# Half 0's last expert groups taken in turns with half 1's first, and half 0's gathered rows added around the wait for the turned gates

## The reference

```
x = x + 0.5 * rwkv_ffn(layernorm(x))
x = x +       softmax_attention(layernorm(x))      # 8 heads
x = x + 0.5 * rwkv_ffn(layernorm(x))
x = x + 0.5 * experts(layernorm(x))                # "m3" in the kernel
x = x +       linear_attention(layernorm(x))       # decayed delta scan, 8 heads
x = x + 0.5 * experts(layernorm(x))                # "m5"
```

```
topk_w, topk_idx = top_k(softmax(x @ Wr + br), 2)   # 16 experts, the best 2 of each token
h = gelu(layernorm(x @ W1[e] + b1[e]) * g1[e] + be1[e])
y = sum over the 2 experts of topk_w * (h @ W2[e] + b2[e])
```

## Time and profile before

| | us |
|---|---|
| median of 3 runs | 601.48 (598.48 to 602.64) |
| the profiled execution | 601.2 |
| its span, first to last instruction | 599.0 |
| PE busy | 487.4 (81%) |
| DVE busy | 468.1 (78%) |
| ACT busy | 312.5 (52%) |
| POOL busy | 158.8 (27%) |
| mean granted PE clock | 0.925 of full |

### The profile page before, as it was taken

The page is one execution under the profiler, slowest core; times in us unless marked ns, Lnnn a source line. Parts: engine busy times, 40 slices in busy tenths (PEclk is TensorE's granted clock), DMA queues, the critical chain, the costliest instruction groups (busy, mean ns, idle before and its releaser), DMA issues.

```text
span 599.0 us, 9248 instructions
## 1 busy us (share of the span) xinstructions
PE 487.4 (81%) x2996; PEld 259.4 (43%) x2996; DVE 468.1 (78%) x1248; ACT 312.5 (52%) x613; POOL 158.8 (27%) x198
## 2 busy tenths in 40 slices
PE   6787989999999999899788789748786887789720
PEld 3452422222222232244364679535435444679610
DVE  4978898988878988465887978697977776888852
ACT  2355456777776777688232658527143202468800
POOL 5020030010000110001274702773101055630775
PEclk8888999999999999999987979987989888999975
DMA  6006500049705003000235295511000012454542
GB/s 209 3 1 162 96 2 0 19 103 194 259 2 146 2 0 72 2 0 2 67 131 163 82 277 162 154 48 27 2 1 0 2 36 68 145 166 139 155 127 66
DMA packets 55356, 49.31 MB, mean 82 GB/s; under 512 B 4958, under 2 KB 47502, under 8 KB 54926
## 3 DMA queue, kind: packets, MB, share of 16 engines
q1 hardware_dynamic: 34686, 31.15, 18.8%
q0 software_dynamic: 4240, 9.45, 5.7%
q10 hardware_dynamic: 16384, 8.13, 4.5%
HBM read 25.85 MB, written 20.59 MB: 78 GB/s over the span
## 4 chain that ended last, share of the span: by engine, by line
PE 37%; DVE 28%; POOL 11%; issue 9%; ACT 9%; DMA 4%; ACTq 1%; SPq 0%; POOLq 0%; DVEq 0%
PE ps L814 9%; DVE arena L862 8%; PE ps L804 7%; PE ps L761 7%; POOL rows_in L1157 7%; ACT arena L1357 5%; POOL arena L1173 2%; DVE stat L257 2%; ACT arena L1366 1%; POOL small L249 1%; DMA row<-in_rows 1%; PE ps L575 1%; DVE arena L1905 1%; DMA arena<-rows_in 1%; DVE xl L285 1%
## 5 line engine op out<-in xcount | busy, mean ns | idle before, releaser
L862 DVE TENSOR_REDUCE arena<-ps 128x1 f32<-128x1024 f32 x128 | 150.8, 1219 | 25.0 <-PE ps L761 24.7
L927 ACT ACTIVATE arena<-ps 128x512 f32<-128x512 f32 x256 | 138.4, 602 | 55.1 <-PE ps L804 52.8
L804 PE MATMUL ps<-arena 99*128 99x512 bf16 x256 | 85.5, 383 | 1.1 <-ACT arena L927 1.0
L761 PE MATMUL ps<-arena 96*128 96x512 bf16 x256 | 76.5, 381 | 7.0 <-DVE arena L862 6.7
L1173 POOL DMA_INDIRECT arena<-rows_out,route x64 | 61.2, 956 | 66.4 <-DMA rows_out<-arena 47.1
L1157 POOL DMA_INDIRECT rows_in<-xl,route x64 | 62.4, 976 | 55.2 <-DVE route L1113 37.1
L814 PE MATMUL ps<-arena 128*32 128x512 f32 x512 | 68.2, 605 | 1.9 <-ACT arena L923 1.3
L804 PEld LDWEIGHTS ps<-arena 99*128 99x128 bf16 x256 | 22.2, 98 | 72.9 <-ACT arena L927 48.9
L249 POOL TENSOR_TENSOR small<-small,nhalf 128x8 f32<-128x8 f32 x11 | 18.2, 1657 | 123.4 <-DVE small L271 123.3
L1357 ACT ACTIVATE arena<-ps,route 128x128 f32<-128x128 f32 x124 | 46.4, 461 | 5.7 <-PE ps L1238 5.7
L202 PE MATMUL ps<-zerob 128*128 128x512 bf16 x148 | 43.7, 448 | 1.4 <-POOL zerob L2100 1.4
(11 more groups left out here) (276 smaller groups left out, 786.6 us busy)
## 6 DMA issues: line engine op xcount, KB each, us to landing
arena<-rows_in SPq DMA_DIRECT2D x28, 256.0 KB, 4.5
rows_out<-arena ACTq DMA_DIRECT2D x28, 256.0 KB, 2.6
rows_in<-zerob SPq DMA_DIRECT2D x2, 1920.0 KB, 11.1
arena<-att_parts SPq DMA_DIRECT2D x12, 256.0 KB, 8.9
arena<-in_consts SPq DMA_DIRECT2D x2, 1024.0 KB
arena<-zerob SPq DMA_DIRECT2D x1, 2048.0 KB, 10.5
arena<-att_parts SPq DMA_DIRECT2D x14, 128.0 KB, 8.1
att_parts<-arena SPq DMA_DIRECT2D x6, 256.0 KB
```

The lines of the kernel that those rows point to most:

```text
L761: ins = pe.matmul(ps[:, bank + keys, :], a_qs[0:96, b, h, j * P:(j + 1) * P], a_ks[0:96, b, h, keys * 512:(keys + 1) * 512], start=True, s ...
L804: pe.matmul(ps[:, score_bank(n), :], a_ks[0:99, b, h0 + h4, i * P:(i + 1) * P], a_qs[0:99, b, h0 + h4, half * 512:(half + 1) * 512], start ...
L862: nc.vector.tensor_reduce(a_nm[:, o % 2, k:k + 1], ps[:, bank:bank + 2, :].rearrange("p a b -> p (a b)"), AX.X, ALU.max, negate=True).then ...
L927: nc.scalar.activation(a_p[:, n % 16, :], ps[:, score_bank(n), :], ACT.Exp, scale=0.25).then_inc(a.ex, 1)
```

## The change

In `moe_tensor` and `moe_scalar` the loop is split at group 8. Up to group 4 it is as before. Then come three rounds: on PE `out(4+k)`, `turn(5+k)`, `turn_in(8+k)`, `hidden(8+k)`; on ACT `out_in(4+k)`, `store(3+k)`, `rows(8+k)`, `gelu(5+k)`, for k = 0, 1, 2. Then half 0's last group is finished (`out(7)`, `out_in(7)`, `store(7)`) ahead of `turn_in(11)` and `rows(11)`, and half 1 goes on in the old loop. `moe_vector_tiles` takes 7 and 8 apart: each has its own chain. Both stages run this code.

Behind the groups of m3, `moe_vector_b2` is split: after the gate rows DVE adds quarters 0 and 1 of half 0's gathered rows, then copies the turned gates, adds quarters 2 and 3, and adds the b2 product last. A semaphore `b2a` tells PE that this last addition is done. On POOL the root for half 0 stands ahead of half 1's gather number 4 instead of 6. Behind m5 the order is as it was.

```diff
--- before.py
+++ after.py
@@ -1006,6 +1006,7 @@
             hot, count = sem("e_one_hot"), sem("e_counts")
             base, slot, tab = sem("e_bases"), sem("e_slots"), sem("e_tile_table")
             turned, pick = sem("e_bases_turned"), sem("e_tile_one_hot")
+            b2a = sem("e_b2_added")
             gw, gwt, gwc, gb = sem("e_gate_rows"), sem("e_gate_rows_turned"), sem("e_gate_rows_in"), sem("e_b2_by_gates")
             gs, gsel = sem("e_scales_summed"), sem("e_scales_in")
             rows_sent = [sem(f"e_rows_sent{b}") for b in range(B)]
@@ -1274,17 +1275,30 @@
             between(1)
             keep_clock(pe, HIDDEN_BANKS[3], 6)
             pe.wait_ge(pair[1].slot, pair[1].i + 1)
-            for u in range(u0, last - LEAD):
+            n = u0 + NGR
+            for u in range(u0, n - LEAD):
                 hidden(u + LEAD)
-                if u + LEAD + 1 < last and u + LEAD + 1 != u0 + NGR:
+                if u + LEAD + 1 < n:
                     turn_in(u + LEAD + 1)
                 turn(u)
                 if u == u0:
                     counts_read(pair[1])
                 else:
                     out(u - 1)
-                if u + LEAD + 1 == u0 + NGR:
+            for k in range(LEAD):
+                out(n - 4 + k)
+                turn(n - 3 + k)
+                turn_in(n + k)
+                hidden(n + k)
+            out(n - 1)
+            turn_in(n + LEAD)
+            for u in range(n, last - LEAD):
+                hidden(u + LEAD)
+                if u + LEAD + 1 < last:
                     turn_in(u + LEAD + 1)
+                turn(u)
+                if u > n:
+                    out(u - 1)
             out(last - LEAD - 1)
             turn(last - 3)
             turn(last - 2)
@@ -1306,7 +1320,7 @@
                     ins = pe.matmul(ps[:, b2_bank(m.b, q), :], r_gt[:, m.b, :], b2d[:, 4 * q:4 * q + 4, :], start=True, stop=True)
                 ins.then_inc(Moe.gb, 1)
 
-        def moe_vector_b2(dve, vs, pair):
+        def moe_vector_gate_rows(dve, vs, pair):
 
             for m in pair:
                 dve.wait_ge(m.gate, m.i + 1)
@@ -1314,6 +1328,8 @@
                     ins = nc.vector.tensor_tensor(r_oh[m.b][:, k], r_oh[m.b][:, k], bc(r_e[m.b][:, k, :].unsqueeze(2), [P, TB, NE]), ALU.mult)
                 vs.step(ins)
                 nc.vector.tensor_tensor(r_oh[m.b][:, 0], r_oh[m.b][:, 0], r_oh[m.b][:, 1], ALU.add).then_inc(Moe.gw, 1)
+
+        def moe_vector_gate_rows_in(dve, pair):
             turn = pair[1].i // B + 1
             dve.wait_ge(Moe.gwt, turn)
             nc.vector.tensor_copy(r_gt[:, :, :], ps[:, TURN_IN_BANKS[0], 0:B * P].rearrange("p (b t) -> p b t", b=B)).then_inc(Moe.gwc, 1)
@@ -1326,7 +1342,8 @@
             for q in range(2):
                 xq = x[:, TB * m.b + 4 * q:TB * m.b + 4 * q + 4, :]
                 ins = nc.vector.tensor_tensor(xq, xq, ps[:, b2_bank(m.b, q), :].rearrange("p (a b) -> p a b", a=4), ALU.add)
-            vs.step(ins)
+            ins.then_inc(Moe.b2a, 1)
+            dve.wait_ge(Moe.b2a, m.i + 1)
 
         def turn_bank(left):
 
@@ -1373,16 +1390,32 @@
             def store(u):
                 moe_scalar_store(act, pair[(u - u0) // NGR], (u - u0) % NGR)
 
-            for u in range(u0, last - LEAD):
+            n = u0 + NGR
+            for u in range(u0, n - LEAD):
                 if u >= u0 + 2:
                     store(u - 2)
-                if u + LEAD + 1 < last and u + LEAD + 1 != u0 + NGR:
+                if u + LEAD + 1 < n:
                     rows(u + LEAD + 1)
                 gelu(u)
                 if u > u0:
                     out_in(u - 1)
-                if u + LEAD + 1 == u0 + NGR:
+            for k in range(LEAD):
+                out_in(n - 4 + k)
+                store(n - 5 + k)
+                rows(n + k)
+                gelu(n - 3 + k)
+            store(n - 2)
+            out_in(n - 1)
+            store(n - 1)
+            rows(n + LEAD)
+            for u in range(n, last - LEAD):
+                if u >= n + 2:
+                    store(u - 2)
+                if u + LEAD + 1 < last:
                     rows(u + LEAD + 1)
+                gelu(u)
+                if u > n:
+                    out_in(u - 1)
             out_in(last - 4)
             store(last - 5)
             gelu(last - 3)
@@ -1432,12 +1465,13 @@
                     bc(t_rs[:, at, pos:pos + k].unsqueeze(2), [P, k, P]), ALU.mult).then_inc(t.z, 1)
 
             last = u0 + 2 * NGR - 1
-            for u in range(u0 - 1, last + 1, 2):
-                groups = range(max(u, u0), min(u + 1, last) + 1)
+            n = u0 + NGR
+            for groups in ([u0], [u0 + 1, u0 + 2], [u0 + 3, u0 + 4], [u0 + 5, u0 + 6], [u0 + 7],
+                           [n], [n + 1, n + 2], [n + 3, n + 4], [n + 5, n + 6], [n + 7]):
                 for v in groups:
                     summed(v)
                 dve.wait_ge(t.ss, groups[-1] + 1)
-                if u < u0:
+                if groups[0] == u0:
                     vs.finish_both(slots, Chain(rstds(groups[0], groups[-1])))
                 else:
                     vs.finish(Chain(rstds(groups[0], groups[-1])))
@@ -1574,6 +1608,7 @@
             def turn(self, g):
                 bank = self.bank("turn", g)
                 self.pe.wait_ge(self.m.added, 4 * self.m.i + 2 * g + 2)
+                self.pe.wait_ge(Moe.b2a, self.m.i + 1)
                 for j in range(4):
                     ins = self.pe.transpose(ps[:, bank, j * P:(j + 1) * P], x[:, TB * self.b + 4 * g + j, :], cc("ident"))
                 ins.then_inc(l.tp, 1)
@@ -2133,7 +2168,7 @@
             moe_pool_send(pool, m3[0])
             moe_pool_send(pool, m3[1])
             moe_pool_fetch(pool, m3[0])
-            moe_pool_fetch(pool, m3[1], {6: lambda: norm_pool_root(pool, n4, 0)})
+            moe_pool_fetch(pool, m3[1], {4: lambda: norm_pool_root(pool, n4, 0)})
             norm_pool_root(pool, n4, 1)
             norm_pool_root(pool, n5, 0)
             moe_pool_send(pool, m5[0], {13: lambda: norm_pool_root(pool, n5, 1)})
@@ -2298,9 +2333,11 @@
                 vs.advance(slots)
 
             def behind_m3():
-                moe_vector_b2(dve, vs, m3)
+                moe_vector_gate_rows(dve, vs, m3)
+                moe_vector_add(dve, vs, m3[0], (0, 1))
+                moe_vector_gate_rows_in(dve, m3)
+                moe_vector_add(dve, vs, m3[0], (2, 3))
                 moe_vector_b2_add(dve, vs, m3[0])
-                moe_vector_add(dve, vs, m3[0])
                 norms = Chain(norm_vector_stats(dve, vs, n4, 0, False, False))
                 for _ in range(VARIANCE_DONE):
                     vs.advance(norms)
@@ -2310,7 +2347,8 @@
             slots = lin_vector(dve, vs, m3, n4, n5, m5)
 
             def behind_m5():
-                moe_vector_b2(dve, vs, m5)
+                moe_vector_gate_rows(dve, vs, m5)
+                moe_vector_gate_rows_in(dve, m5)
                 for m in m5:
                     moe_vector_b2_add(dve, vs, m)
                 moe_vector_add(dve, vs, m5[0])
```

## The result

The changed kernel takes 604.01 us (median of 22 runs, 600.8 to 607.71) against 601.62 (22 runs, 598.13 to 603.95): ratio **1.0046, 95% interval 1.0028 to 1.0064**, by which it is 2.8 us (1.7 to 3.9) slower; the medians lie 2.4 apart. The forecast was 602.1, +0.9. Direction and mechanism came as forecast; the size did not.

What follows compares the result with a forecast made beforehand. The prediction took POOL's queue and group 15's store to bound the end: -2.5 us behind m3 and +4.1 in the second stage put half 1's gathers at 574.3 instead of 573.42, +0.9, 602.1 us; range 597.8 to 606.2.

Steps and rivals of the forecast that it cites:

- The end hangs on POOL's queue and group 15's store: Second stage's end: POOL free at 573.4, group 15's store plus 2.8 at 572.7; earlier half 0 wins at most 0.7 us.
- A round takes 4.2 us: PE and ACT, groups 5 to 7: nothing runs under gelu, so a group takes 4.2 us instead of 3.05.
- Second stage: Second expert stage: DVE 4.0 us late at group 10's statistics, last store 4.1 late; half 0's last store 0.55 earlier.
- First stage: First expert stage: group 10's statistics at 361.0 against 360.35, 0.6 us late; half 0's last store 3.9 earlier.
- Behind m3, 2.5 us earlier: After the first stage: row adds fill DVE's waits, root moves on POOL; linear attention starts at 395.9 instead of 398.44.
- The sum: Whole kernel: last store 569.88 - 2.5 + 4.1 = 571.5, half 1's gathers at 574.3; +0.9 us, 602.1.
- The additional chain costs nothing: DVE, groups 7 and 8 apart: about 3.15 us a chain, covered by the wait for hidden(10); price between 0 and 3.1.
- Rival, the clock lost in the rounds: PE at half speed in the rounds: 604.6 for one stage, chance 0.20; 607.1 for both, chance 0.05.
- Rival, half 1 is not late: PE and ACT overlap more in a round, group 10's statistics come in time: end moves -3.0, 598.2; chance 0.15.
- the gain behind m3 does not arrive: Gathers late for quarters 2 and 3, or linear attention gives it back: up to 2.5 us lost, 604.6; chance 0.10.

Runs made afterwards that it cites:

- the rounds alone: The changed kernel with `moe_vector_b2` in one piece and POOL's root ahead of gather 6, as before the change: 607.07 us, ratio 1.0099 to the kernel before.
- the tail alone: The changed kernel with PE, ACT and DVE taking groups in the old order, new only behind m3's groups: 599.93 us, 0.9953; on the third chip 682.99, 0.9989.
- rounds in stage 1 alone: The changed kernel with the old group order on PE, ACT and DVE in the second stage: 601.32 us, ratio 1.0001 to the kernel before.

## Why the prediction came out as it did

- **The end hangs on POOL's queue and group 15's store.** Right. The new last store is at 572.82, half 1's gathers start 2.87 later at 575.69, as with the 2.8 taken, and POOL would have been free at 571.3.
- **A round takes 4.2 us.** Right: 4.25 and 4.14, with the waits where they were put.
- **Second stage.** Right: the store of group 15 4.1 late was forecast, 46.95 - 42.63 = 4.3 measured. For half 0's last store 0.55 earlier was forecast; from group 0's store it took 22.59 instead of 23.16, 0.57 less. Group 10's statistics were forecast 4.0 late; from group 0's store they came 547.17 - 525.87 = 21.30 behind instead of 17.33 (544.58 - 527.25), 3.97 late.
- **First stage: group 10's statistics "0.6 late only".** This is the term that was mis-sized. Against before's own trace it was 47.31 - 45.72 = 1.6, and 43.78 - 42.64 = 1.1 from group 1's store, of which 0.75 is group 10's statistics: against its base the term was nearly right. The base was not. It held a long wait for the rows and a fall of the clock, which I noted but took for what the stage always does. In the old order that comes in some executions (two of five stages seen), and such a stage is 3.4 us longer (45.98 - 42.60). With its share, the old order takes 42.60 + 0.4 x 3.4 = 44.0 in the mean, an estimate from five stages, and the rounds cost 47.3 - 44.0 = 3.3 a stage. Two stages give 6.6, less the 0.7 that POOL's queue hides at the end 5.9, where the rounds alone measured 6.0 (4.3 to 7.6). The sum had 0.6 + 4.1 less 0.7, 4.0.
- **Behind m3, 2.5 us earlier.** The mechanism was right: L280 was forecast 9.65 behind group 15's store and came 9.31 behind it, with POOL's queue binding the root. But group 15's store was later than forecast, so that from group 0's store L280 is 56.62 us away instead of 58.51, 1.9 earlier and not 2.5. With the tail alone, DVE's wait of 3.04 us for the last gathers and POOL's of 1.79 for the variance take the place of POOL's queue; its L280 of 395.95 is 2.49 earlier than before, but 1.43 of that it had already at group 15's store.
- **The sum.** +0.9 forecast, from 4.0 for the rounds and -3.1 behind m3. With the parts as the traces give them, 5.9 for the rounds and 12.79 - 9.31 = 3.5 back behind m3, it is 2.4; the change measured 2.8 (1.7 to 3.9). So the rounds were priced 2 us too low and the tail about right. The measurement tells about 1 us from no change, not only 6 us as the prediction has it.
- **The additional chain costs nothing.** Right in the trace; DVE's waits of 2.92 and 1.86 us are what is left behind it.
- **Rival, the clock lost in the rounds.** Did not happen: 1.00 in both seams. In seven stages with the rounds PE had no wait for the rows and no fall, both of which the old order has at times. The Trainium skill, TensorE: Matmul & The Clock Gate, section "Loop structure matters more than you think", says that a VectorE copy out of PSUM between products does not break the clock, while a long wait for a DMA does. The traces of the seams agree in part, though the waits there are for ACT and not for VectorE: no fall behind PE's waits of 0.85 and 1.4 us for ACT, a fall behind 1.94 and 2.36 us for a DMA, none behind DMA waits of 0.30 to 0.93. The waits for ACT were also the shorter ones. And PE waits for DVE at the start of every expert stage, where the clock fell behind 2.48 us of it in before, behind 2.52 with the tail alone and 2.45 with the rounds alone, and not behind 2.69 in the kernel with rounds in stage 1 alone. A wait for an engine can be followed by a fall, and as long a wait in another stage or execution is not.
- **Rival, half 1 is not late.** Did not happen; **the gain behind m3 does not arrive** did not happen where the kernel before takes 601 us. On the two slower chips it did.

What is not shown: what stalls the engines of the second and third chip, how often the clock falls in the old order beyond five stages, and how much of such a stage's 3.4 us is the clock and how much the longer wait.

## What to carry to other kernels

Before filling a wait with other work, price the order that does the filling: on two in-order queues that hand each group back and forth, moving `out(u-1)` out from under `gelu(u)` cost 1.1 to 1.2 us a round for three rounds, to save a wait of 0.3 to 2.4 us once. Work that is only moved earlier into a wait (two quarters of the row adds ahead of the turned gates) was the part that gained, and only as far as its inputs were there: 1.1 us from group 15's store to L280 with the old order of the groups, 3.5 with half 0's gathers earlier. And a stretch of a single profile in which the clock fell is one draw: look at the same stretch of another stage or run before using it as the base of a sum.

## What the runs showed of the hardware

- At the seam the clock fell behind PE waits of 1.94 and 2.36 us for the rows, and not behind 0.93, 0.51 and 0.30; the fall lasted about 6 us, and a stage with the long wait and the fall took 3.4 us more. At the stage's start PE waits 2.4 to 2.7 us for DVE in all twelve stages of the six profiles at about 601 us, and in each profile the clock fell to 0.50 to 0.65 behind one of the two waits and stayed at 1.00 behind the other.
- The same kernel took 601.5 us on one chip and 682.5 and 684 on two others. Pauses of about 5 us and more on PE, ACT and DVE, while POOL issued indirect DMAs, are what the traces of the two slower chips have and the first's don't. The change cost 1.0046 where the kernel before takes 601.6 us and 1.0093 on the third chip, and the gain of its tail, 0.9953 on the first, was 0.9989 (0.9965 to 1.0012) on the third.
